# Two transformer layers on one core: masking the future on GpSimd behind the exponential, in place of triangle matmuls

## What is computed

```python
scores = jnp.einsum('bhqd,bhkd->bhqk', q, k) / jnp.sqrt(jnp.float32(HDIM))
qi = jnp.arange(S)[:, None]
kj = jnp.arange(S + 1)[None, :]
causal = kj <= qi + 1
scores = jnp.where(causal[None, None], scores, jnp.float32(MASK_OUT))
...
attn = jax.nn.softmax(scores, axis=-1)
out = jnp.einsum('bhqk,bhkd->bhqd', attn, v)
```

## Time and profile before

| | |
|---|---|
| median of three runs | 343.66 us (339.81, 343.66, 346.64) |
| the profiled execution | 341.08 us, of which the span is 339.3 us |
| PE busy | 294.3 us (87%), 1888 matmuls |
| DVE busy | 256.6 us (76%) |
| ACT busy | 170.0 us (50%) |
| POOL busy | 28.6 us (8%), 58 instructions |
| mean granted clock of PE | 0.943 of full speed |

### The profile page before, as it was taken

The page is one execution under the profiler, slowest core; times in us unless marked ns, Lnnn a source line. Parts: engine busy times, 40 slices in busy tenths (PEclk is TensorE's granted clock), DMA queues, the critical chain, the costliest instruction groups (busy, mean ns, idle before and its releaser), DMA issues.

```text
span 339.3 us, 5440 instructions
## 1 busy us (share of the span) xinstructions
PE 294.3 (87%) x1888; PEld 149.5 (44%) x1888; DVE 256.6 (76%) x764; ACT 170.0 (50%) x246; POOL 28.6 (8%) x58
## 2 busy tenths in 40 slices
PE   0286874988899999999999999999999999999990
PEld 0134351335544544454433332334444357776770
DVE  5887976999778779999899988887932134665765
ACT  1865540046465666474486756763868721221210
POOL 3061000005060000000000000002100000000101
PEclk9996765599999999999999999999999999999997
DMA  7793157203554006540015440080000000000011
GB/s 174 176 212 74 27 174 177 59 3 122 144 97 81 4 8 193 125 92 2 2 38 177 103 101 0 3 248 2 0 2 2 0 2 0 1 2 0 2 31 32
DMA packets 14991, 22.83 MB, mean 67 GB/s; under 512 B 2222, under 2 KB 12338, under 8 KB 14196
## 3 DMA queue, kind: packets, MB, share of 16 engines
q1 hardware_dynamic: 14676, 22.21, 26.5%
q0 software_dynamic: 288, 0.28, 0.7%
HBM read 13.99 MB, written 4.72 MB: 55 GB/s over the span
## 4 chain that ended last, share of the span: by engine, by line
PE 54%; DVE 15%; issue 11%; DMA 8%; SPq 8%; ACT 2%; POOLq 0%; POOL 0%; DVEq 0%; ACTq 0%
PE ps_pv L1349 14%; PE ps_s L1308 11%; PE ps_t L1331 9%; DVE mx L1029 7%; PE ps_s L1424 6%; PE ps_misc L1437 5%; DMA Ks<-Qs 5%; DVE shared L1025 2%; SPq L521 2%; SPq L508 2%; DVE mx L1025 1%; ACT probs L800 1%; SPq L544 1%; PE ps_t L1334 1%; DMA Ks<-parts_k 1%
## 5 line engine op out<-in xcount | busy, mean ns | idle before, releaser
L800 ACT ACTIVATE probs<-ps_t 128x1024 f32<-128x1024 f32 (+2 forms) x128 | 106.1, 861 | 58.8 <-PE ps_t L1334 27.8
L1029 DVE TENSOR_REDUCE mx<-ps_s 128x1 f32<-128x512 f32 x128 | 81.9, 685 | 10.4 <-PE ps_s L1308 9.9
L1308 PE MATMUL ps_s<-Ks,Qs 128*128 128x512 bf16 (+2 forms) x235 | 75.9, 353 | 10.0 <-DVE mx L1025 3.4
L1331 PE MATMUL ps_t<-Qs,Ks 128*128 128x512 bf16 (+3 forms) x256 | 67.6, 340 | 0.9 <-ACT probs L800 0.7
L1349 PE MATMUL ps_pv<-probs,Vs 128*32 128x512 f32 (+3 forms) x512 | 55.9, 523 | 0.0
L1025 DVE CUSTOM_DVE_ANT_0 shared<-ps_s,shared 128x256 bf16<-128x256 f32 (+3 forms) x107 | 46.4, 461 | 12.3 <-PE ps_s L1308 11.9
L1308 PEld LDWEIGHTS ps_s<-Ks,Qs 128*128 128x128 bf16 x235 | 21.9, 98 | 65.9 <-DVE mx L1029 31.0
L1331 PEld LDWEIGHTS ps_t<-Qs,Ks 128*128 128x128 bf16 x256 | 24.0, 98 | 24.3 <-issue 5.9
L786 ACT ACTIVATE shared<-ps_s,cols 128x512 f32<-128x512 f32 x16 | 11.0, 686 | 40.4 <-PE ps_s L1424 40.4
L1137 DVE SCALAR_TENSOR_TENSOR shared<-ps_misc,comb,shared 128x128 f32<-128x128 f32 x48 | 13.5, 343 | 23.0 <-PE ps_misc L1437 23.0
L1424 PE MATMUL ps_s<-Qf,Ks 128*128 128x512 f32 x64 | 30.4, 597 | 0.0
(11 more groups left out here) (263 smaller groups left out, 330.6 us busy)
## 6 DMA issues: line engine op xcount, KB each, us to landing
parts_q<-Qp SPq DMA_DIRECT2D x20, 128.0 KB, 1.9
Qs<-parts_q SPq DMA_DIRECT2D x24, 96.0 KB
Ks<-parts_k SPq DMA_DIRECT2D x24, 96.0 KB
Qs<-parts_q SPq DMA_DIRECT2D x12, 192.0 KB
Ks<-parts_k SPq DMA_DIRECT2D x12, 192.0 KB
Ks<-Qs SPq DMA_DIRECT2D x2, 1024.0 KB, 12.1
parts_k<-Kp SPq DMA_DIRECT2D x12, 128.0 KB, 1.8
Qs<-Qs SPq DMA_DIRECT2D x1, 1024.0 KB, 12.1
```

Source lines behind the costliest of these rows:

```text
L800: act.activation(probs[:, half % 2, j, 0:w], ps[:, 0:w], ACT.Exp).then_inc(free[f"t{i % 2}"], 1)
L1029: last = dve.tensor_reduce(mx[:, b, t, h:h + 1], ps[:, 0:w], AX, ALU.max)
L1308: mm = pe.matmul(ps[:, 0:w], Qs[:, b, h, t * P:(t + 1) * P], Ks[:, b, h, 0:w], start=True, stop=True)
L1331: mm = pe.matmul(ps[:, col:col + w], Ks[:, b, h, kb * P:(kb + 1) * P], Qs[:, b, h, S - w:S], start=True, stop=(a >= 2))
```

## The change

The triangle matmuls of `attend` and their constant `causal_k` go. In their place POOL, in the same step of the list, waits for ACT's exponential of the unit and sets the probabilities of future keys to zero in place: one `affine_select` on both diagonal squares of the unit, 128 partitions by 2 x 128 fp32 numbers. That makes 32 for each causal attention, 64 in all. PE's `values` for a causal half now wait on the count of these selects (four for each half) in place of ACT's signals. The order of the steps is the same.

```diff
-        causal_k = sb("causal_k", [P, P], bf16)
...
+        future_zeroed = sem("future_zeroed")
...
-                    pool.memset(causal_k[:, :], 0.0)
...
-                    pool.affine_select(out=causal_k[:, :], in_=causal_k[:, :], compare_op=ALU.is_ge, fill=BIG,
-                                       base=0, pattern=[[1, P]], channel_multiplier=-1)
...
+                if step == "attend" and a < 2:
+
+                    r, u, j = unit(i)
+                    half = 2 * (a * ROUNDS + r) + u
+                    pool.wait_ge(free[f"t{i % 2}"], filled(f"t{i % 2}", "weights", a, i))
+                    (_, _, w), _ = blocks_of(a, u)
+                    early_two = probs[:, half % 2, j, 0:2 * w].rearrange("p (k q) -> p k q", k=2)[:, :, 0:P]
+                    pool.affine_select(out=early_two, in_=early_two, compare_op=ALU.is_ge, fill=0.0, base=0,
+                                       pattern=[[0, 2], [1, P]], channel_multiplier=-1).then_inc(future_zeroed, 1)
...
                     for kb, col, w in blocks_of(a, u):
                         mm = pe.matmul(ps[:, col:col + w], Ks[:, b, h, kb * P:(kb + 1) * P],
-                                       Qs[:, b, h, S - w:S], start=True, stop=(a >= 2))
-                        if a < 2:
-                            mm = pe.matmul(ps[:, col:col + P], identb[:, :], causal_k[:, :],
-                                           start=False, stop=True)
+                                       Qs[:, b, h, S - w:S], start=True, stop=True)
...
                         for n in (2 * GROUP * r + GROUP * u + 2, 2 * GROUP * r + GROUP * u + 3):
-                            pe.wait_ge(free[f"t{n % 2}"], filled(f"t{n % 2}", "weights", a, n))
+                            if a >= 2:
+                                pe.wait_ge(free[f"t{n % 2}"], filled(f"t{n % 2}", "weights", a, n))
+                        if a < 2:
+                            pe.wait_ge(future_zeroed, (half + 1) * GROUP)
```

## The result

The changed kernel takes 349.35 us in the median (347.17 to 351.04, four executions), the kernel before 342.47 us beside it (339.81 to 346.64). The ratio is 1.0227, with an interval of 1.018 to 1.0274: 2.3% slower, some 7 us. Four more executions on another chip gave 1.0191 (1.0128 to 1.0253). A time given here is the median of all executions, while a ratio compares fast executions alone, so that it can differ by some tenths of a per cent from the quotient of two medians. The prediction was 344.7 us, 1.9 us slower, in a range of 340 to 351. The range held, and so did the sign; the size did not: it is that of the slow rival, 348.7.

A forecast was written before the change was run, and what follows sets the result against it. The prediction took PE, with DVE close behind, to bound the causal attentions from 77 to 168 us. Triangles -3.0, waits +1.0, POOL's queue +3.3 and casts +0.6 gave +1.9 on 342.8, so 344.7 us, range 340 to 351.

The forecast's parts named there:

- the slow rival: PE's clock falls at the stall behind POOL's transfers, at most 5 us lost, 4 taken: 348.7 us; chance 0.28.
- the likeliest case: Whole kernel: triangle gain, added waits, POOL's stall and held-up casts sum to +1.9 us, no clock fall; chance 0.50.
- POOL's queue: Nine transfers between selects of units 22 and 23 of a = 0 hold POOL 5.29 us; PE stalls: +3.3 us.
- The clock: PE's clock falling at the stall near 112 us: nothing in the sum, kept as a rival with chance 0.28.
- The triangles: Dropping 128 triangle matmuls from PE in the causal attentions: -3.0 us, 2.0 for a = 0, 1.0 for a = 1.
- The select: One POOL select on two 128 x 128 squares takes 0.50 us; exponential to `values` becomes 0.80 us.
- the four close halves: Causal halves with `values` 0.46 to 0.72 us behind the exponential; each should show a short wait on POOL.
- The waits and casts: PE's added waits for selects at close halves, +1.0 us; DVE's casts held up by POOL's selects, +0.6 us.
- The sum: Whole kernel: -3.0 + 1.0 + 3.3 + 0.6 = +1.9 us, set on a mean of 342.8 us: 344.7 us.
- The stated 0.17 for slower by over 2%: Chance of a time over 350.5 us, said to need both the clock's fall and dear selects.

The follow-up runs named there:

- six transfers: Changed kernel with six of nine small transfers left between the 23rd and 24th select, three behind the last causal select: 345.67 us, ratio 1.0075 to the kernel before.
- late transfers: Changed kernel with POOL's nine small transfers issued behind the last causal select, not between the 23rd and 24th: 342.41 us, ratio 1.0017 to the kernel before.
- Masking twice: Kernel before with its triangle matmuls plus the 64 selects and PE's waits for them, nine transfers issued behind the last causal select: 342.41 us, ratio 1.0020.

## Why the prediction was right in part

The time lies within the range because the range was drawn wide enough for the slow rival, not because the likeliest case was right. That case, +1.9 us, missed on two terms, and both misses point the same way: the clock was left out and the triangles were taken for too much.

- **POOL's queue, +3.3 us: right.** The transfers began when the select of unit 22 was done, held POOL 5.29 us (107.74 to 113.03), and PE waited 3.07 us. The stall alone costs 2.8 us.
- **The clock, 0 in the sum: this is the step that failed.** The forecast took "at most 5 us lost, 4 taken" into a rival of 0.28 and not into the likeliest case. The mechanism, its place and, within what can be told, its price were those of the rival: 4.3 and 3.1 us by the ratios, 3.4 and 2.3 by the traces. What the prediction put against it, that PE is dense on both sides here, did not hold the clock up: it fell in both profiled executions of the changed kernel, and in the one with six transfers 1.1 us after a wait of 1.49 us. The late transfers, with the same work and no stall, kept it at 1.00. What it put behind it, that dense work makes the low spell short, held: 10.2 and 6.8 us. The Trainium skill, "TensorE: Matmul & The Clock Gate", Part 1, named there, says that the clock drops to half after idling and comes back once PE is busy. Both traces of the changed kernel agree, with 10.2 and 6.8 us at half clock by PE's one long wait; the falls at 70 to 73 us in other traces, with no idle time over 0.35 us ahead, are not explained by it.
- **The triangles, -3.0 us: about twice too much, if not more.** Leaving them out gave 1.3 us (0.9962), and 0.3 us between the first and the last exponential. The step took the shares of L1334 on the chain, 2.0 us for a = 0, for time that comes back. A share of the chain is what an engine did while it was the last one; it does not say how far behind the next one is, and here DVE's maxima and the signals to them were as good as level. The 3.0 us lie just outside what leaving them out can have given, 2.9 us at the most.
- **The select, 0.50 us: near.** It takes 0.41 to 0.42. The whole way from exponential to `values` is 0.53 us at the half that ends with unit 23, when the transfers are late, and 0.62 us at the closest of the four close halves, where 0.80 was forecast. So they missed less: one of them shows a wait for POOL, of 0.20 us, where short waits at all four were to be seen.
- **The waits and casts, +1.0 and +0.6: about right, within what can be told.** Masking twice costs 0.7 us (up to 1.7, which is also what its trace shows). The difference between late transfers with selects (1.0017) and neither mask (0.9962) is 1.9 us, with wide intervals. The casts behave as the earlier trace rows said: beside selects L999 took 0.62 us and L1006 0.51 and 0.54, in place of 0.43, in the changed kernel, 0.38 us in all.
- **The sum.** With the measured parts in it, -1.3 + 0.7 + 2.8 + 4.3 = +6.5 us for the first measurement and +5.3 with the 3.1 of the second, where 7.8 and 6.5 were measured (0.0227 and 0.0191 of 342 us). What is left is within the intervals. This proves less than it seems to, since the last two terms are themselves differences of the measured ratios. What it tests is that -1.3 + 0.7 = -0.6 us should be the time of the version with late transfers, which is +0.6 (from -1.1 to +2.2).
- **The stated 0.17 for slower by over 2%** was too low for the same reason: with the fall in the likeliest case, the stall and the fall make 7 us together, right at the bound.

## What to carry to other kernels

An engine with 8% busy is not free: what already stands in its queue, a few transfers that nobody waits for, becomes a wait of the bounding engine once work of the main path is queued behind it, so read that queue in program order and put such things where the trace shows a gap. A wait of some us on PE is to be costed with the clock that it may take along, here about as much again as the wait itself. And before taking work off one engine of a close pair, leave it out altogether once: that bound, 1.3 us here for 7.1 us of matmuls, tells whether anything can be won.

## What the runs showed of the hardware

- The clock fell at the two waits of 3.07 us, and once 1.1 us after a wait of 1.49 us in an otherwise dense stretch (six transfers).
- Four traces, all without triangles, have short falls of 3.4 us besides: at 70.0 to 73.0 us in all four, and in three of them a second one at 138.3, 140.8 and 144.3 us. The second stands each time at the end of an idle time of PE, or up to 0.4 us behind it, at one and the same place of its order: 0.91, 1.28 and 1.51 us; in the other ten traces PE is idle there for 0.84 us or less, and the clock does not fall. From unit 31 of a = 0 to the last exponential of a = 3 these three take 155.3 to 155.7 us, the five other traces without triangles 153.4 to 153.7. The length of the wait does not decide alone, as waits of 1.00 to 1.31 us at 79 to 93 us had no fall.
- In none of the five traces with triangle matmuls does the clock fall again, once it has risen at 67 to 75 us, until the attentions are over. That the triangles keep it up is not shown: the first of them comes at 77.53 us in the kernel before, behind the time of the falls at 70 to 73 us, which therefore have another cause.
- Issuing the nine small transfers held POOL's queue for 5.29 to 5.31 us wherever they stood: 95.10 to 100.39, 107.74 to 113.03 and 86.75 to 92.06 us. A select behind them started only then.
- On DVE a plain reduction of 128 x 512 and a sum with maximum of the same size take the same time, 0.686 and 0.689 us; the second has 0.082 us for the accumulator behind it.
